# Self-attention: the order of TensorE's work over two key tiles, and the lag of the weighings

## The chip, the cores and the metric

The program runs on one core of one Trainium2 chip. The metric is the device time of one execution in microseconds. The engines are TensorE (PE, matmuls; PEld is its weight load), VectorE (DVE), ScalarE (ACT), GpSimd (POOL) and SyncE (SP, which issues DMAs). Each runs its own queue in order and waits for semaphores of the others.

## The reference

The kernel computes two decoder layers on x (4 x 1024 tokens, width 256): cross-attention to 64 context tokens, self-attention with a mixture of experts, cross-attention again, and a second mixture of experts. The change is in the self-attention alone:

```python
q = (src @ q_w).reshape(b, s, h, hd).transpose(0, 2, 1, 3)
k = (src @ k_w).reshape(b, s, h, hd).transpose(0, 2, 1, 3)
v = (src @ v_w).reshape(b, s, h, hd).transpose(0, 2, 1, 3)
scores = jnp.einsum('bhqd,bhkd->bhqk', q, k) / np.float32(np.sqrt(hd))
scale = jax.nn.sigmoid(jnp.einsum('bhsd,hd->bhs', q, scale_w)) * 2.0
scores = scores * scale[..., None]
aw = jax.nn.softmax(scores, axis=-1)
out = jnp.einsum('bhqk,bhkd->bhqd', aw, v).transpose(0, 2, 1, 3).reshape(b, s, d)
```

Here b = 4, s = 1024, h = 16, hd = 16.

## The kernel before

The stages of the program are separate blocks that run one after the other. An earlier stage stores queries (with their scale) and keys in bf16 parts. `self_attention` takes 16 groups of four heads (one batch each) and halves the queries of a group: 32 units of 512 queries by 1024 keys by 4 heads. `n` is the unit, `kt` its key tile (8 tiles of 128 keys), `head` 0 to 3.

In a unit each engine does this:

- TensorE, scores (line 1137): for each key tile and head one matmul, 128 keys by 512 queries, over 112 partitions, into one of three PSUM buffers `bps`. The partitions hold the bf16 parts of queries and keys and two rows with the negated maximum of each query, so the maximum is already taken off. There are four a tile.
- ScalarE, exponentials (line 1086): one for each of these, out of PSUM into `ex`, of which there are two buffers, one for each key tile in turn.
- TensorE, weighings (line 1147, `weigh_values`): once a tile, the four heads' 17 columns of values (16 and a column of ones for the sum) times their exponentials. The heads stand side by side in 32 columns of the array each, and each fp32 matmul shows as two instructions, so eight a tile. They add up in the one buffer `ops` over the unit.
- TensorE, maxima (line 1106, `first_scores`): rougher scores of a unit to come, 128 queries by 1024 keys, on 48 partitions. Two heads run at a time, one on partitions 0 to 47 and one on 64 to 111, into one of two buffers `aps`. VectorE takes the maximum of each (line 1020). A unit needs 16 such steps, two a tile; they run a unit and more ahead (`ahead` says for which).
- In tile 3 (`MAX_AT`) TensorE transposes the next unit's maxima (line 1118), ScalarE copies them negated (line 1064), GpSimd splits them (line 982) and SyncE sends them through memory into the rows of the queries.
- When a unit's last weighing is done, ScalarE copies `ops` (line 1056, `keep_out`) in the next unit's first tile. In tile 5 (`OUT_AT`) TensorE transposes the copy (line 1127), ScalarE copies the result (line 1072) and GpSimd divides (line 993).

The order of each queue is written out by hand in the `body` of each engine. On TensorE a tile is: score 0, two maximum steps, a transpose if one is due, score 1, the weighing of the tile before, scores 2 and 3. The transposes use the same three PSUM buffers as the scores, in turn (`b_use`). Semaphores of the part: `b_filled` (a score buffer is written), `b_used` (ScalarE has read it), `a_filled` and `a_used` (the same for maxima), `pv_done` (weighings done), `o_evacuated` (`ops` copied). A score waits for the exponential three buffers back:

```python
def fill(use):
    if use >= 3:
        pe.wait_ge(b_used, use - 2)
```

Of the kernel before, what the change touches and what calls it, by code (L numbers as in the profile page):

```python
# [13 lines left out]
P = 128  # L14
# [8 lines left out]
CW = CT * P  # L23
# [557 lines left out]
GH = 4  # L581
# [268 lines left out]
def self_attention(nc, attn, ident, q_parts, k_parts, v_dram, m_dram, x_sb, n2_b):  # L850
# [10 lines left out]
    MAX_AT, OUT_AT = 3 * GH + 1, 5 * GH + 1  # L861

# [18 lines left out]
    with ExitStack() as ctx:  # L881
# [5 lines left out]
        ex = [sb(f"e{i}", [P, GH, CW]) for i in range(2)]  # L887
# [30 lines left out]
        with nc.Block() as block:  # L918
# [133 lines left out]
            def _(act):  # L1052
# [21 lines left out]
                def body(g, turn, s, turn1, s1):  # L1074
                    for qc in range(2):
                        n = 2 * g + qc
                        for i in range(GH * KT):
# [19 lines left out]
            def _(pe):  # L1097
# [42 lines left out]
                def weigh_values(n, kt, s, turn):  # L1140
# [5 lines left out]
                    for head in range(GH):  # L1146
                        last = nc.tensor.matmul(ops[32 * head:32 * head + VW], vs[s][:, kt, head], ex[kt % 2][:, head],  # L1147
                                                start=(kt == 0), stop=(kt == KT - 1))
                    last.then_inc(pv_done, 1)

                def body(g, turn, s, turn1, s1):
                    for qc in range(2):
                        n = 2 * g + qc
                        for kt in range(KT):
                            scores(n, GH * kt, s, turn, qc)
                            for which in range(2):
                                if ahead(n, kt, which):
                                    a, k = ahead(n, kt, which)
                                    if kt < 2 and qc == 0:
                                        first_scores(a, k, s, turn, 1)  # L1160
                                    else:
                                        first_scores(a, k, s1, turn1, 0 if kt < 2 else qc)
                            if GH * kt + 1 == MAX_AT and n + 1 < UNITS:
                                transpose_max(n + 1)
                            if GH * kt + 1 == OUT_AT and n >= 1:
                                transpose_out(n)
                            scores(n, GH * kt + 1, s, turn, qc)
                            if kt:
                                weigh_values(n, kt - 1, s, turn)
                            elif qc:  # L1170
                                weigh_values(n - 1, KT - 1, s, turn)
                            elif g >= 1:
# [1497 lines left out]
```

## Time and profile before

| | us |
|---|---|
| median of 3 runs | 2056.4 (2055.46 to 2056.41) |
| the profiled execution, its own time | 2058.98 |
| its span | 2056.9 |
| TensorE, VectorE, ScalarE, GpSimd busy over the span | 1713.4, 1250.0, 969.1, 603.5 |
| scores: 1024 matmuls | 311.1 |
| weighings: 2048 | 270.4 |
| maxima: 1024 matmuls, 512 reductions | 168.2, 602.3 |
| exponentials: 1024 | 534.5 |

A matmul's time in the profile is from its start to a modelled end, and neighbours overlap. So the distance from start to start says what one costs TensorE, not the duration. Reductions and exponentials overlap their neighbours in the same way, a little. A row that groups several instructions gives the start of the first and the time that all together cover.

### The profile page before, as it was taken

What the parts mean: (1) busy time and instruction counts of PE and PEld (TensorE: products, weight loads), DVE (VectorE), ACT (ScalarE), POOL (GpSimd) and SP (SyncE); (2) the same over time, 40 slices, a digit from 0 to 9 for tenths busy, and PEclk for the clock granted to TensorE, in tenths of its full rate; (3) what the DMA queues carried; (4) which work ended last, traced back from release to release, by engine and by line L of the source; (5) the groups of instructions that cost most, each with busy time, mean ns of one, the idle gap of its engine ahead of it and who ended that gap; (6) DMA issues with size and microseconds to landing.
All of it is one profiled execution on the core that took longest, in us unless ns stands there. A gap on an engine that the chain in (4) does not pass through costs nothing. (4 is left out here: it accounts for less than half of the span.)

```text
span 2056.9 us, 30275 instructions
## 1 busy us (share of the span) xinstructions
PE 1713.4 (83%) x10579; PEld 808.6 (39%) x10580; DVE 1250.0 (61%) x2123; ACT 969.1 (47%) x1811; POOL 603.5 (29%) x645
## 2 busy tenths in 40 slices
PE   5799799389999999999997884999077996329997
PEld 3466455012222222222221563776044663125654
DVE  5344344588888888888881484665783554562221
ACT  3422256158888888888887331444242332102110
POOL 4300034613222122121122264666561001120533
PEclk9899989679999999999999995999588998758998
DMA  5000048711221111321100622221400003310542
GB/s 138 1 2 1 16 156 288 208 38 38 55 56 38 38 38 38 67 45 37 38 2 1 220 80 85 59 69 56 125 1 1 1 1 124 135 32 11 124 122 31
DMA packets 112675, 134.48 MB, mean 65 GB/s; under 512 B 18481, under 2 KB 88497, under 8 KB 112273
## 3 DMA queue, kind: packets, MB, share of 16 engines
q1 hardware_dynamic: 101824, 114.20, 20.5%
q0 software_dynamic: 9552, 17.83, 3.6%
q8 instruction: 86, 1.41, 0.3%
q10 hardware_dynamic: 1152, 0.54, 0.1%
q14 instruction: 61, 0.49, 0.1%
HBM read 78.47 MB, written 53.93 MB: 64 GB/s over the span
## 5 line engine op out<-in xcount | busy, mean ns | idle before, releaser
L1020 DVE TENSOR_REDUCE sa_mhalf<-sa_a 128x2 f32<-128x1024 f32 x512 | 602.3, 1221 | 86.8 <-PE sa_a L1106 86.8
L1086 ACT ACTIVATE sa_e<-sa_b 128x512 f32<-128x512 f32 x1024 | 534.5, 601 | 139.4 <-PE sa_b L1137 139.4
L1137 PE MATMUL sa_b<-sa_q,sa_k 112*128 112x512 bf16 x1024 | 311.1, 385 | 3.2 <-ACT sa_e L1086 3.0
L1147 PE MATMUL sa_ops<-sa_e,sa_v 128*17 128x512 f32 x2048 | 270.4, 599 | 6.3 <-ACT sa_e L1086 1.1
L1137 PEld LDWEIGHTS sa_b<-sa_q,sa_k 112*128 112x128 bf16 x1024 | 78.8, 97 | 322.6 <-ACT sa_e L1086 281.6
L1106 PE MATMUL sa_a<-sa_k,sa_q 48*128 48x512 bf16 x1024 | 168.2, 398 | 38.4 <-DMA sa_k<-k_parts 24.5
L993 POOL TENSOR_TENSOR sa_rden<-sa_o_rows,sa_minus_one 128x16 f32<-128x16 f32 x32 | 93.1, 2908 | 180.1 <-ACT sa_o_rows L1072 180.1
L213 DVE TENSOR_REDUCE xa_mx<-xa_rows 128x16 f32<-128x1024 f32 x64 | 78.3, 1224 | 102.6 <-PE xa_rows L445 102.6
L982 POOL CAST sa_negm<-sa_neg 16x128 bf16<-16x128 f32 x32 | 9.0, 281 | 380.1 <-issue 338.0
L1106 PEld LDWEIGHTS sa_a<-sa_k,sa_q 48*128 48x128 bf16 x1024 | 42.1, 93 | 177.6 <-issue 77.0
L360 ACT ACTIVATE xa_pT<-xa_cols 128x1024 f32<-128x1024 f32 x64 | 62.1, 1021 | 84.9 <-PE xa_cols L477 84.9
L2552 DVE TENSOR_TENSOR sw_hT<-sw_p,sw_act 128x512 f32<-128x512 f32 x32 | 22.1, 692 | 101.9 <-PE sw_p L2497 101.9
L2465 POOL DMA_INDIRECT out_x<-sw_yo,tc_idx x32 | 49.9, 1560 | 105.5 <-DVE sw_yo L2559 98.5
L1637 PE MATMUL ex_hps<-at_w,ex_xT 128*128 x156 | 77.3, 619 | 1.9 <-ACT ex_xT L1677 1.9
L445 PE MATMUL xa_rows<-xa_kblk,xa_qT 64*128 64x256 f32 x512 | 73.1, 407 | 6.1 <-DVE xa_mx L213 5.3
L2541 ACT ACTIVATE sw_act<-sw_p 128x512 f32<-128x512 f32 x32 | 19.1, 597 | 118.8 <-PE sw_p L2491 110.3
L1660 PE MATMUL ex_yps<-at_attn,ex_hT 128*128 x312 | 74.1, 380 | 0.5 <-ACT ex_hT L1687 0.4
L544 PE MATMUL xa_cols<-c_ctxT,c_wts 128*128 128x256 f32 x16 | 7.5, 652 | 78.0 <-PEq L43 64.5
L1687 ACT ACTIVATE ex_hT<-ex_tps,at_bt,at_g 128x128 f32<-128x128 f32 x156 | 58.8, 457 | 15.7 <-PE ex_tps L1648 15.7
L726 POOL TENSOR_TENSOR sp_var<-sp_mv,x_eps_pow 128x4 f32<-128x4 f32 x8 | 7.5, 939 | 190.7 <-DVE sp_mv L683 190.7
L2491 PE MATMUL sw_p<-sw_xT,tc_w 128*128 128x512 f32 x128 | 62.0, 608 | 1.2 <-ACT sw_xT L2530 1.2
L1147 PEld LDWEIGHTS sa_ops<-sa_e,sa_v 128*17 128x17 f32 x2048 | 34.9, 95 | 69.5 <-ACT sa_e L1086 48.8
(328 smaller groups left out, 2819.7 us busy)
## 6 DMA issues: line engine op xcount, KB each, us to landing
k_parts<-sp_kpart SPq DMA_DIRECT2D x96, 128.0 KB, 1.8
sa_q<-q_parts SPq DMA_DIRECT2D x64, 192.0 KB, 5.1
sa_k<-k_parts SPq DMA_DIRECT2D x64, 192.0 KB, 5.6
tc_w<-in_L_ffn_W SPq DMA_DIRECT2D x24, 512.0 KB
q_parts<-sp_qpart SPq DMA_DIRECT2D x16, 384.0 KB, 3.3
ex_xg<-expert_in SPq DMA_DIRECT2D x39, 132.0 KB
v_groups<-sp_vt SPq DMA_DIRECT2D x8, 544.0 KB, 4.1
sa_v<-v_groups SPq DMA_DIRECT2D x16, 272.0 KB, 7.3
```

The source lines that it names most:

```text
L213: nc.vector.tensor_reduce(mx[:, t], rows[:].rearrange("p r (n k) -> p (r n) k", k=SC), axis=X, op=ALU.max).then_inc(max_done, 1)
L360: nc.scalar.activation(pT[:, 4 * half + 2 * part:4 * half + 2 * part + 2], cols[:, 2 * part:2 * part + 2], ACT.Exp, scale=SCALE).then_inc( ...
L445: last = nc.tensor.matmul(rows[:, r, half * D:(half + 1) * D], qT[part, half, tokens], kblk[part, c // 2, half, CT * r:CT * (r + 1)], star ...
L993: nc.gpsimd.tensor_tensor(rden[:], view[:, :, :, DK], minus_one[:], ALU.pow).then_inc(rden_made, 1)
L1020: nc.vector.tensor_reduce(mhalf[a % 2][:, half, head:head + PAIRED + 1:PAIRED, t], aps[use % 2][:], axis=X, op=ALU.max).then_inc(a_used, 1)
L1086: nc.scalar.activation(ex[kt % 2][:, head], bps[use % 3][:], ACT.Exp, scale=SCALE).then_inc(b_used, 1)
L1106: last = nc.tensor.matmul(aps[use % 2][:, h // PAIRED], qs[s][rows, h, q0:q0 + P], ks[s][rows, h, half * CW:(half + 1) * CW], start=True, ...
L1137: nc.tensor.matmul(bps[use % 3][:], ks[s][:, head, kt * P:(kt + 1) * P], qs[s][:, head, qc * CW:(qc + 1) * CW], start=True, stop=True).the ...
L1147: last = nc.tensor.matmul(ops[32 * head:32 * head + VW], vs[s][:, kt, head], ex[kt % 2][:, head], start=(kt == 0), stop=(kt == KT - 1))
L1637: last = nc.tensor.matmul(hps[j % 2][:], xT[j % 2][:, half], ew["w1"][:, half, ds(e, 1), :], start=(half == 0), stop=(half == HALVES - 1))
L1660: last = nc.tensor.matmul(yps[j % 2][:, 0:D], hT[j % 2][:, f], ew["w2"][:, f, ds(e, 1), :], start=(f == 0), stop=(f == FK - 1))
L2491: last = nc.tensor.matmul(p1[f % 2][:], w1[e % 3][:, half, f * P:(f + 1) * P], xT[e % 2][:, half], start=(half == 0), stop=(half == HALVES ...
```

## The change

TensorE's order is written for two tiles at a time, and the weighing of a tile comes two tiles behind its exponentials (`LAG = 2`) in place of one. In an even tile: scores 0 and 1, the weighing, one maximum step, scores 2 and 3. In an odd tile: score 0, one maximum step, the weighing, a transpose if one is due, scores 1 and 2, two maximum steps, score 3. A third buffer of exponentials takes the tile more that is under way, and ScalarE's wait before it writes one goes one weighing further back. The copy of `ops` moves with the last weighing, from behind the second exponential of a unit to behind its sixth. Behind the last unit two weighings are left in place of one. What is computed, and how many instructions of each kind, is the same.

```diff
+    LAG = 2
...
-        ex = [sb(f"e{i}", [P, GH, CW]) for i in range(2)]
+        ex = [sb(f"e{i}", [P, GH, CW]) for i in range(LAG + 1)]
...
-                            if head == 0 and n >= 1 or kt >= 2 and head == 0:
-                                act.wait_ge(pv_done, KT * n + kt - 1)
+                            if head == 0 and KT * n + kt > LAG:
+                                act.wait_ge(pv_done, KT * n + kt - LAG)
                             act.wait_ge(b_filled, use + 1)
-                            nc.scalar.activation(ex[kt % 2][:, head], bps[use % 3][:], ACT.Exp, scale=SCALE).then_inc(b_used, 1)
-                            if i == 1 and n >= 1:
+                            nc.scalar.activation(ex[(KT * n + kt) % (LAG + 1)][:, head], bps[use % 3][:], ACT.Exp, scale=SCALE).then_inc(b_used, 1)
+                            if i == GH + 1 and n >= 1:
                                 keep_out(n)
...
-                            scores(n, GH * kt, s, turn, qc)
-                            for which in range(2):
-                                if ahead(n, kt, which):
...
-                            if GH * kt + 1 == MAX_AT and n + 1 < UNITS:
-                                transpose_max(n + 1)
-                            if GH * kt + 1 == OUT_AT and n >= 1:
-                                transpose_out(n)
-                            scores(n, GH * kt + 1, s, turn, qc)
-                            if kt:
-                                weigh_values(n, kt - 1, s, turn)
...
-                            for head in range(2, GH):
-                                scores(n, GH * kt + head, s, turn, qc)
+                            def maxima(pairs):
+                                for p in pairs:
+                                    if ahead(n, kt // 2 * 2 + p // 2, p % 2):
...
+                            if kt % 2 == 0:
+                                scores(n, GH * kt, s, turn, qc)
+                                scores(n, GH * kt + 1, s, turn, qc)
+                                weigh()
+                                maxima((0,))
+                                scores(n, GH * kt + 2, s, turn, qc)
+                                scores(n, GH * kt + 3, s, turn, qc)
+                            else:
+                                scores(n, GH * kt, s, turn, qc)
+                                maxima((1,))
+                                weigh()
+                                if GH * kt + 1 == MAX_AT and n + 1 < UNITS:
+                                    transpose_max(n + 1)
+                                if GH * kt + 1 == OUT_AT and n >= 1:
+                                    transpose_out(n)
+                                scores(n, GH * kt + 1, s, turn, qc)
+                                scores(n, GH * kt + 2, s, turn, qc)
+                                maxima((2, 3))
+                                scores(n, GH * kt + 3, s, turn, qc)
...
-                weigh_values(UNITS - 1, KT - 1, (GROUPS - 1) % SETS, (GROUPS - 1) // SETS)
+                for kt in range(KT - LAG, KT):
+                    weigh_values(UNITS - 1, kt, (GROUPS - 1) % SETS, (GROUPS - 1) // SETS)
```

TensorE in two plain tiles, before. `sa_b` is a score buffer, `sa_a` one of the maxima, `sa_ops` the weighing's, `sa_e` the exponentials that it reads; the numbers are those of the buffers.

```order
L1137 MATMUL sa_b0<-sa_q1,sa_k1 128x512
L1106 MATMUL sa_a0<-sa_k2,sa_q2 128x512 x2
L1106 MATMUL sa_a1<-sa_k2,sa_q2 128x512 x2
L1137 MATMUL sa_b1<-sa_q1,sa_k1 128x512
L1147 MATMUL sa_ops<-sa_e1,sa_v1 17x512 x4
L1137 MATMUL sa_b2<-sa_q1,sa_k1 128x512
L1137 MATMUL sa_b0<-sa_q1,sa_k1 128x512
L1137 MATMUL sa_b1<-sa_q1,sa_k1 128x512
L1106 MATMUL sa_a0<-sa_k2,sa_q2 128x512 x2
L1106 MATMUL sa_a1<-sa_k2,sa_q2 128x512 x2
L1137 MATMUL sa_b2<-sa_q1,sa_k1 128x512
L1147 MATMUL sa_ops<-sa_e0,sa_v1 17x512 x4
```

The same place now, from score 0 of an odd tile to the first maximum step of the even tile behind it (lines are one higher).

```order
L1138 MATMUL sa_b1<-sa_q1,sa_k1 128x512
L1107 MATMUL sa_a1<-sa_k2,sa_q2 128x512 x2
L1148 MATMUL sa_ops<-sa_e2,sa_v1 17x512 x4
L1138 MATMUL sa_b2<-sa_q1,sa_k1 128x512
L1138 MATMUL sa_b0<-sa_q1,sa_k1 128x512
L1107 MATMUL sa_a0<-sa_k2,sa_q2 128x512 x2
L1107 MATMUL sa_a1<-sa_k2,sa_q2 128x512 x2
L1138 MATMUL sa_b1<-sa_q1,sa_k1 128x512
L1138 MATMUL sa_b2<-sa_q1,sa_k1 128x512
L1138 MATMUL sa_b0<-sa_q1,sa_k1 128x512
L1148 MATMUL sa_ops<-sa_e0,sa_v1 17x512 x4
L1107 MATMUL sa_a0<-sa_k2,sa_q2 128x512 x2
```

The weighing stands beside a maximum step on both tiles' sides, and the score right ahead of the even tile's weighing (the last `sa_b0`) writes the buffer that the second score behind the odd tile's weighing (the first `sa_b0`) has filled.

ScalarE from the copy of the transposed output in one unit (L1072) to the negated maxima in the next (L1064), before:

```order
L1072 ACTIVATE sa_o_rows<-sa_b 128x512
L1086 ACTIVATE sa_e<-sa_b 128x512 x13
L1056 ACTIVATE sa_o<-sa_ops 128x512
L1086 ACTIVATE sa_e<-sa_b 128x512 x11
L1064 ACTIVATE sa_neg<-sa_b 16x128
```

And now:

```order
L1073 ACTIVATE sa_o_rows<-sa_b 128x512
L1087 ACTIVATE sa_e<-sa_b 128x512 x17
L1057 ACTIVATE sa_o<-sa_ops 128x512
L1087 ACTIVATE sa_e<-sa_b 128x512 x7
L1065 ACTIVATE sa_neg<-sa_b 16x128
```

The copy of `ops` (L1056, now L1057) has moved four exponentials back, into the unit's tile 1.

## Rows read from the trace of the kernel before

**Rows 1.** The page, part 1: busy time, share of the span, instructions.

```profile
PE 1713.4 (83%) x10579; PEld 808.6 (39%) x10580; DVE 1250.0 (61%) x2123; ACT 969.1 (47%) x1811; POOL 603.5 (29%) x645
```

**Rows 2.** Busy time by stretch; below, all matmuls of line 1106.

```profile
core 0: us, PE busy (x) PEld busy (x) DVE busy (x) ACT busy (x) POOL busy (x), PEclk, DMA share, GB/s
500.00:1000.00 500.00, 496.79 (x3046) 121.84 (x3043) 435.73 (x389) 405.61 (x802) 109.08 (x97) 1.00 0.22 43
...
L1106 PE MATMUL sa_a<-sa_k,sa_q x1024: 376/386/631, 392.4 to 1085.0; 48*128 48x512 bf16 x171
```

**Rows 3.** Timeline of TensorE, tiles 2 and 3 of a unit.

```profile
start us, us, engine line op out<-in xcount [idle before <-releaser]
...
693.64 0.82 PE L1137 MATMUL sa_b<-sa_q,sa_k 112*128 112x512 bf16 x3
694.39 0.61 PE L1106 MATMUL sa_a<-sa_k,sa_q 48*128 48x512 bf16 x4
694.93 0.39 PE L1137 MATMUL sa_b<-sa_q,sa_k 112*128 112x512 bf16 x1
695.25 1.05 PE L1147 MATMUL sa_ops<-sa_e,sa_v 128*17 128x512 f32 x8
696.24 0.82 PE L1137 MATMUL sa_b<-sa_q,sa_k 112*128 112x512 bf16 x3
696.99 0.64 PE L1106 MATMUL sa_a<-sa_k,sa_q 48*128 48x512 bf16 x4
697.56 0.28 PE L1118 MATMUL sa_b<-x_ident,sa_mfull 128*16 128x128 f32 x1
697.80 0.39 PE L1137 MATMUL sa_b<-sa_q,sa_k 112*128 112x512 bf16 x1
698.12 1.05 PE L1147 MATMUL sa_ops<-sa_e,sa_v 128*17 128x512 f32 x8
699.11 0.82 PE L1137 MATMUL sa_b<-sa_q,sa_k 112*128 112x512 bf16 x3
```

**Rows 4.** Waits from 440 to 1080 us: who waited for whom, total, times, longest.

```profile
PEld sa_b L1137 <- ACT sa_e L1086: 255.3, 413, 0.9
```

**Rows 5.** Timeline of the last unit, which has no maxima left.

```profile
1099.30 1.05 PE L1147 MATMUL sa_ops<-sa_e,sa_v 128*17 128x512 f32 x8
...
1100.28 0.82 PE L1137 MATMUL sa_b<-sa_q,sa_k 112*128 112x512 bf16 x3
...
1100.71 2.06 ACT L1086 ACTIVATE sa_e<-sa_b 128x512 f32<-128x512 f32 x4 [0.48 <-PE sa_b L1137]
...
1101.36 0.39 PE L1137 MATMUL sa_b<-sa_q,sa_k 112*128 112x512 bf16 x1 [0.26 <-ACT sa_e L1086]
...
1101.85 1.05 PE L1147 MATMUL sa_ops<-sa_e,sa_v 128*17 128x512 f32 x8
```

**Rows 6.** Timeline of VectorE at the tiles of rows 3; the page's group of line 1020.

```profile
694.83 2.36 DVE L1020 TENSOR_REDUCE sa_mhalf<-sa_a 128x2 f32<-128x1024 f32 x2 [0.27 <-PE sa_a L1106]
697.42 2.36 DVE L1020 TENSOR_REDUCE sa_mhalf<-sa_a 128x2 f32<-128x1024 f32 x2 [0.24 <-PE sa_a L1106]
...
L1020 DVE TENSOR_REDUCE sa_mhalf<-sa_a 128x2 f32<-128x1024 f32 x512 | 602.3, 1221 | 86.8 <-PE sa_a L1106 86.8
```

**Rows 7.** Timeline of TensorE in the second cross-attention, at two places.

```profile
1618.26 1.13 PE L445 MATMUL xa_rows<-xa_kblk,xa_qT 64*128 64x256 f32 x8
1619.32 1.92 PE L486 MATMUL xa_front<-xa_pT,xa_vblk 128*32 128x512 f32 x16
...
1618.80 0.60 PE L445 MATMUL xa_rows<-xa_kblk,xa_qT 64*128 64x256 f32 x4
...
1653.74 1.13 PE L445 MATMUL xa_rows<-xa_kblk,xa_qT 64*128 64x256 f32 x8
1654.80 1.92 PE L486 MATMUL xa_front<-xa_pT,xa_vblk 128*32 128x512 f32 x16
```

**Rows 8.** Timeline of ScalarE, then TensorE, around the output's transpose, tile 5.

```profile
702.13 1.08 ACT L1086 ACTIVATE sa_e<-sa_b 128x512 f32<-128x512 f32 x2 [0.53 <-PE sa_b L1137]
...
703.72 0.60 ACT L1072 ACTIVATE sa_o_rows<-sa_b 128x512 f32<-128x512 f32 x1
704.22 0.59 ACT L1086 ACTIVATE sa_e<-sa_b 128x512 f32<-128x512 f32 x1
...
701.71 0.82 PE L1137 MATMUL sa_b<-sa_q,sa_k 112*128 112x512 bf16 x3
...
703.03 0.66 PE L1127 MATMUL sa_b<-x_ident,sa_o 128*128 128x128 f32 x4
703.52 0.38 PE L1137 MATMUL sa_b<-sa_q,sa_k 112*128 112x512 bf16 x1
...
704.82 0.39 PE L1137 MATMUL sa_b<-sa_q,sa_k 112*128 112x512 bf16 x1
```

**Rows 9.** Timeline of ScalarE and TensorE around the output copy.

```profile
712.78 0.60 ACT L1056 ACTIVATE sa_o<-sa_ops 128x512 f32<-128x512 f32 x1 [0.24 <-PE sa_ops L1147]
713.27 2.06 ACT L1086 ACTIVATE sa_e<-sa_b 128x512 f32<-128x512 f32 x4
...
712.64 0.82 PE L1137 MATMUL sa_b<-sa_q,sa_k 112*128 112x512 bf16 x3
...
715.48 0.39 PE L1137 MATMUL sa_b<-sa_q,sa_k 112*128 112x512 bf16 x1
```

**Rows 10.** Line 1056 between 690 and 760 us: count, durations, first and last start.

```profile
L1056 ACT ACTIVATE sa_o<-sa_ops x4: 597/598/598, 690.9 to 756.5; 128x512 f32<-128x512 f32 x4
```

**Rows 11.** The first weighing, timeline of TensorE, and busy times and clock there.

```profile
430.10 1.91 PE L1147 MATMUL sa_ops<-sa_e,sa_v 128*17 128x512 f32 x8
431.94 0.89 PE L1137 MATMUL sa_b<-sa_q,sa_k 112*128 112x512 bf16 x3
...
429.00:432.50 3.50, 3.50 (x16) 0.48 (x12) 2.53 (x3) 1.13 (x3) 0.00 (x0) 0.55 0.00 0
```

**Rows 12.** Timeline of TensorE at the end of the stage.

```profile
1125.46 1.05 PE L1147 MATMUL sa_ops<-sa_e,sa_v 128*17 128x512 f32 x8 [0.96 <-ACT sa_e L1086]
1127.23 0.66 PE L1127 MATMUL sa_b<-x_ident,sa_o 128*128 128x128 f32 x4 [0.72 <-ACT sa_o L1056]
```

**Rows 13.** Timeline of ScalarE at the tiles of rows 3.

```profile
696.66 1.57 ACT L1086 ACTIVATE sa_e<-sa_b 128x512 f32<-128x512 f32 x3 [0.53 <-PE sa_b L1137]
```

More of the change, by code:

```diff
@@ L1146, in weigh_values @@
                     for head in range(GH):
-                        last = nc.tensor.matmul(ops[32 * head:32 * head + VW], vs[s][:, kt, head], ex[kt % 2][:, head],
+                        last = nc.tensor.matmul(ops[32 * head:32 * head + VW], vs[s][:, kt, head], ex[(KT * n + kt) % (LAG + 1)][:, head],
                                                 start=(kt == 0), stop=(kt == KT - 1))
@@ L1154, in body @@
                         for kt in range(KT):
-                            scores(n, GH * kt, s, turn, qc)
-                            for which in range(2):
-                                if ahead(n, kt, which):
[L1158 to L1162, printed above, removed]
@@ L1163, in body @@
-                            if GH * kt + 1 == MAX_AT and n + 1 < UNITS:
-                                transpose_max(n + 1)
-                            if GH * kt + 1 == OUT_AT and n >= 1:
-                                transpose_out(n)
-                            scores(n, GH * kt + 1, s, turn, qc)
-                            if kt:
-                                weigh_values(n, kt - 1, s, turn)
-                            elif qc:
-                                weigh_values(n - 1, KT - 1, s, turn)
-                            elif g >= 1:
-                                weigh_values(n - 1, KT - 1, (s - 1) % SETS, turn)
@@ L1174, in body @@
-                            for head in range(2, GH):
-                                scores(n, GH * kt + head, s, turn, qc)
+                            def maxima(pairs):
+                                for p in pairs:
+                                    if ahead(n, kt // 2 * 2 + p // 2, p % 2):
+                                        a, k = ahead(n, kt // 2 * 2 + p // 2, p % 2)
+                                        if kt < 2 and qc == 0:
+                                            first_scores(a, k, s, turn, 1)
+                                        else:
+                                            first_scores(a, k, s1, turn1, 0 if kt < 2 else qc)
@@ new lines, in weigh @@
+                            def weigh():
+                                if kt >= LAG:
+                                    weigh_values(n, kt - LAG, s, turn)
+                                elif qc:
+                                    weigh_values(n - 1, KT + kt - LAG, s, turn)
+                                elif g >= 1:
+                                    weigh_values(n - 1, KT + kt - LAG, (s - 1) % SETS, turn)
+                            if kt % 2 == 0:
[5 more added lines that the diff above has]
+                                scores(n, GH * kt + 3, s, turn, qc)
+                            else:
+                                scores(n, GH * kt, s, turn, qc)
[9 more added lines that the diff above has]
+                                scores(n, GH * kt + 3, s, turn, qc)
```

## Prediction, made before the changed kernel ran

> Short names: s is one score matmul (line 1137), A one maximum step (two matmuls of line 1106 side by side), W one weighing (eight of line 1147), M and T the transposes of lines 1118 and 1127. s0E to s3E are the scores of an even key tile, s0O to s3O those of an odd one.
>
> **What bounds the kernel now.** I read the page's busy shares first, then the self-attention stretch alone, then the order of instructions in one key tile, and last the release of each wait. Over the whole span no engine is full, but in the 500 us inside self-attention TensorE is busy 496.8 us at full clock, VectorE 435.7, ScalarE 405.6 [rows 1, 2]. The stage's first matmul of maxima starts at 392.4 and its last transpose at 1127.2 [rows 2, 12]; its neighbours are separate blocks, so what it gains or loses moves the end one for one.
>
> A plain key tile repeats every 2.60 us (693.64 to 696.24), and TensorE's starts account for all of it [rows 3]. Three s then A: 0.75. The three s span 0.82 with a last one of 0.38, so s to s is 0.22 and s to A 0.31. The pair of A spans 0.61 with 0.38 each, so A to A is 0.23 and A to s 0.54 - 0.23 = 0.31. s to W is 0.32 and W to s 0.99; the second half of W starts 0.45 after the first in a 1.05 span of 0.60 each, so about 0.10 of the 0.99 is not streaming. Sum: 0.44 + 0.31 + 0.23 + 0.31 + 0.32 + 0.99 = 2.60. Thus each change of kind costs about 0.09 to 0.10 above the 0.22 that neighbours of one kind take, four times a tile. The table of waits blames ScalarE for 255 us before the scores [rows 4]; that is weight loading that stands behind W, not an idle TensorE, as the 496.8 us show.
>
> A second loop is almost as long: W waits for the tile's last exponential, s2 comes after W, and its exponential 0.43 after s2. Where no maxima are left it is alone and takes 2.55 (1099.30 to 1101.85) [rows 5]. So the lag of two frees a path that is only 0.05 shorter than TensorE's own. VectorE has slack: two reductions take 2.36 and it idles 0.24 before the next two [rows 6].
>
> **The change, part by part.** *TensorE's order.* Two tiles before: four s to s, two s to A, two A to A, two A to s, two s to W, two W to s = 0.88 + 0.62 + 0.46 + 0.62 + 0.64 + 1.98 = 5.20. After: s0E s1E W A s2E s3E s0O A W s1O s2O A A s3O. That is five s to s (1.10), s to W 0.32, W to A, A to s 0.31, s to A 0.31, A to W, W to s 0.99, s to A 0.31, A to A 0.23, A to s 0.31. Eight changes of kind before, eight after. Two boundaries are not in this loop's trace. A to W: in cross-attention, pairs of matmuls on 64 rows are followed by four at a time on 32 columns, the same two layouts. The last two pairs (x4, span 0.60, one 0.38) start 0.22 apart and the next kind 0.52 after the first of them, which leaves 0.30 to 0.31 [rows 7]; from the first of the four pairs it is 1.06 in both places shown. Bounds: 0.23 (A to A, nothing extra) and 0.32 (s to W). I take 0.31. W to A: bounds 0.89 (two halves of 0.45, nothing extra) and 0.99 (W to s); above, one more 0.10. I take 0.99, since every other change of kind pays. Sum 5.18: the new order itself wins 0.02 in two tiles. VectorE keeps up with it: a reduction starts 0.44 after its A (694.39, 694.83) and the next 1.14 behind (2.36 - 1.22) [rows 3, 6], so the first two, with A at 1.53 and 2.59, start at 1.97 and 3.11; the second ends at 4.33, before the last A at 4.65 that writes its buffer.
>
> *The lag and the third buffer.* W no longer waits for ScalarE and ScalarE's guard on the buffers is a weighing long past: nothing on the path. But the score buffers are still three. s1 of an even tile may only be written when the exponential of s2O is done, and s2O stands close behind s1O, right after W. Chain from s1E: W 0.32, A 0.99, s2E 0.31, s3E and s0O 0.44, A 0.31, W 0.31, s1O 0.99 = 3.67; exponential of s1O 0.43 later, that of s2O 0.48 behind it (two span 1.08, one 0.60) [rows 5, 8], its length 0.60, and 0.05 until the score matmul that waits for it (1100.71 + 0.60 to 1101.36) [rows 5]. Total 5.23. That beats 5.18 and is 0.03 over 5.20: **+0.03 per two tiles, +0.12 per unit** of eight.
>
> The Trainium skill's page TensorEngine Tiling (Array Packing), section PSUM Bottleneck, says that packing speeds up TensorE but not the emptying of PSUM. The trace agrees so far: 5.18 on TensorE stands against 5.23 on ScalarE's side.
>
> *The output copy* (line 1056) moves from behind the exponential of s1E in tile 0 to behind that of s1O in tile 1. There it sits inside the chain just named: copy to next exponential is 0.49 (712.78 to 713.27) [rows 9], so the exponential of s2O, and s1 of tile 2 with it, come 0.49 later. Before, the copy cost that unit 0.24: the tile from 712.64 to 715.48 takes 2.84 [rows 9]. **+0.25 per unit.** Its own wait is gone (0.24 idle [rows 9]), since s1O comes 0.99 after W; that wins nothing, for the exponential it stands behind starts later than W ends.
>
> *M* at tile 3: before 2.87 against 2.60, +0.27 [rows 3]; after it stands between W and s1O and adds M to s, 0.24. **-0.03.**
>
> *T* at tile 5: before the tile takes 3.11 (701.71 to 704.82), +0.51 [rows 8]. After, T to s adds 0.49. Then ScalarE copies the rows 0.69 after T's start and takes 0.50 to the next exponential, at 1.19; that exponential could have started 0.49 + 0.43 = 0.92 after T. The 0.27 was absorbed before, behind W; now it lies in the chain: 0.76. **+0.25.**
>
> Sum per unit: 0.12 + 0.25 - 0.03 + 0.25 = +0.59. Units 1 to 29 of 32 have all of it: 29 x 0.59 = **+17.1**. A unit before is (756.5 - 690.9) / 3 = 21.87 us long, from four output copies [rows 10].
>
> *Ends.* In unit 0 the first W leaves tile 1, where W to s took 1.84, with a granted clock of 0.55, so mostly at the level of 1.2 GHz [rows 11], and nothing of the output costs applies: **-1.8**. The maxima there are held by VectorE, so I take no more. From tile 2 of unit 30 on there are no A, seven tile pairs. Before 5.10 each [rows 5]; after, the chain from s1E to s1O is 0.32 + 0.99 + 0.44 + 0.32 + 0.99 = 3.06, plus 1.56 = 4.62: 7 x -0.48 = -3.4. The dearer output copy and T, two of each, give back 2 x 0.25 + 2 x 0.25 = 1.0: **-2.4**. The final second W fits into the 0.96 that TensorE idles for the last exponential [rows 12].
>
> Total 17.1 - 1.8 - 2.4 = +12.9. The profiled execution took 2058.98 us (span 2056.9 and 2.1 around it) and would take 2071.9; the timed runs have the median 2056.4, so I put **2069.3 us**. About 0.2% (4 us) is what a measurement of this kernel can tell from no change.
>
> **The rivals.** *A: W and A next to each other cost no change.* Then W to A is 0.89 and A to W 0.23, 0.18 less per two tiles; 121 such pairs have both, 12.9 - 21.8 = -8.9: 2047.5 us. For it: both are packed layouts and W now waits for nothing. Against it: rows 7; and s to W reads 0.32 even behind M, where the exponential it needs, the second of 696.66, ended about 0.4 us earlier (W at 698.12) [rows 3, 13]. The Trainium skill's page TensorE: Matmul & The Clock Gate, section The mechanism (Part 3), says that weight loads are pulled ahead of running matmuls when row groups do not conflict or the background buffer is free. By that, weights would be loaded early and this rival's time holds. Its page TensorEngine Tiling (Array Packing), section Key Properties, says instead that changing the tiling mode drains the engine; by that my 0.31 and 0.99 hold, and rows 7 stand on that side.
>
> *B: only one of the two is free.* -0.10 or -0.08 on 121 pairs: 12.9 - 11 = about +2: 2058.3, no change.
>
> *C: the chain over the three score buffers does not bind,* because exponentials release earlier than I read. Then TensorE's 5.18 sets the pace and output copy and row copy are hidden: 4 x 5.18 + 0.24 + 0.49 = 21.45 against 8 x 2.60 + 0.24 + 0.27 + 0.51 = 21.82 a unit, 29 x -0.37 = -10.7. Seven pairs without A take 6 x 0.22 + 2 x 0.32 + 2 x 0.99 = 3.94 for 5.10, -8.1, unit 0 -1.8: -20.6, 2035.8 us. Against it: rows 5 show just this release, 0.05 behind the exponential.
>
> *D: W to A costs one change more, A to W too.* +0.20 on 121 pairs: +24, 2093.5 us. Only that no row shows W to A speaks for it.
>
> **How the numbers follow.** Forecast 0.78, A 0.07, B 0.06, C 0.04, D 0.05. The forecast's own spread is 2063 to 2076: 0.05 us in either direction on the chain of two tiles is 6 us. Range 2057 to 2078: it takes in B and leaves A, C and D out. Faster 0.11; same 0.08 (B and the low edge of the forecast); slower 0.81.
>
> **What would show it.** Right: eight changes of kind in two tiles, W to A near 0.99 and A to W near 0.31; two plain tiles at 5.2, the even short (about 2.3) and the odd long (about 2.9); an idle of TensorE before s1 of tile 2, about 0.5 behind the output copy, and one behind T; unit 22.4 us; weighings never waiting; the last unit shorter by 1 to 2 us. Wrong: A to W near 0.23, or no idle of TensorE before s1 of the even tiles, or maxima waiting for VectorE in the doubled place (A A), which by rows 6 have over 0.2 us to spare.

## The result and the profile after

The changed kernel took 2065.72 us, median of 7 runs (2063.00 to 2068.61), against 2056.40 for the kernel before (7 runs). The ratio is 1.0050, interval 1.0038 to 1.0062: slower, by 9.3 us. The forecast was 2069.3 us, range 2057 to 2078. One execution of a later run, e5_short_exp_before, took 4343.41 us where its others took 2029.01 to 2030.16; it counts as slow and is left out there.

The spans of the two profiled executions differ by 7.0 us (2056.9, 2063.9), the self-attention stage by more. From its first maximum matmul to its last transpose it took 1127.23 - 392.4 = 734.8 us before [rows 2, 12] and takes 1134.10 - 387.7 = 746.4 now: +11.6. The stages ahead of it, whose code did not change, happened to take 4.7 us less in this execution, those behind it 0.1 more. So the stage is the steadier measure, and below each run is also given by it. It is not free of chance either: how much of its first unit falls before TensorE's clock rises moves it by about 1 us (see *Unit 0* below).

Line 1107 in the trace after (all its matmuls: min, median, max, first and last start), and the end of the stage in TensorE's timeline:

```profile
L1107 PE MATMUL sa_a<-sa_k,sa_q x1024: 376/386/631, 387.7 to 1096.2; 48*128 48x512 bf16 x171
...
1132.33 1.05 PE L1148 MATMUL sa_ops<-sa_e,sa_v 128*17 128x512 f32 x8 [0.25 <-ACT sa_e L1087]
1134.10 0.66 PE L1128 MATMUL sa_b<-x_ident,sa_o 128*128 128x128 f32 x4 [0.72 <-ACT sa_o L1057]
```

The stretch of [rows 2], after: TensorE is busy 489.41 of 500 us and not 496.79, at the same full clock, and the other engines do less as well.

```profile
500.00:1000.00 500.00, 489.41 (x2981) 114.53 (x2977) 424.56 (x381) 400.11 (x783) 108.35 (x95) 1.00 0.22 42
```

TensorE's timeline from tile 5 of one unit to tile 0 of the next answers to [rows 3]:

```profile
704.04 0.66 PE L1128 MATMUL sa_b<-x_ident,sa_o 128*128 128x128 f32 x4
704.54 0.60 PE L1138 MATMUL sa_b<-sa_q,sa_k 112*128 112x512 bf16 x2
705.07 0.61 PE L1107 MATMUL sa_a<-sa_k,sa_q 48*128 48x512 bf16 x4
705.60 1.15 PE L1138 MATMUL sa_b<-sa_q,sa_k 112*128 112x512 bf16 x3
706.69 1.05 PE L1148 MATMUL sa_ops<-sa_e,sa_v 128*17 128x512 f32 x8
707.67 0.39 PE L1107 MATMUL sa_a<-sa_k,sa_q 48*128 48x512 bf16 x2
707.99 0.82 PE L1138 MATMUL sa_b<-sa_q,sa_k 112*128 112x512 bf16 x3
708.75 0.39 PE L1107 MATMUL sa_a<-sa_k,sa_q 48*128 48x512 bf16 x2
709.07 1.05 PE L1148 MATMUL sa_ops<-sa_e,sa_v 128*17 128x512 f32 x8
710.05 0.60 PE L1138 MATMUL sa_b<-sa_q,sa_k 112*128 112x512 bf16 x2
710.59 0.61 PE L1107 MATMUL sa_a<-sa_k,sa_q 48*128 48x512 bf16 x4
711.13 0.88 PE L1138 MATMUL sa_b<-sa_q,sa_k 112*128 112x512 bf16 x3
711.94 1.05 PE L1148 MATMUL sa_ops<-sa_e,sa_v 128*17 128x512 f32 x8
712.92 0.39 PE L1107 MATMUL sa_a<-sa_k,sa_q 48*128 48x512 bf16 x2
```

Both unseen boundaries are there. Weighing to maximum step: 706.69 to 707.67, 0.98. Maximum step to weighing: 708.75 to 709.07, 0.32. So neighbours of these two kinds pay for the change like all others. Two plain tiles take 5.25 (707.67 to 712.92). Three scores in a row span 0.82 where nothing holds them (707.99), 0.88 ahead of the even tile's weighing (711.13) and 1.15 behind the output's transpose (705.60). What is over 0.82 is TensorE waiting for a score buffer.

Before the change two plain tiles took 5.23, not twice the 2.60 of [rows 3]: 704.82 to 707.42 is 2.60, 707.42 to 710.05 is 2.63.

```profile
704.82 0.82 PE L1137 MATMUL sa_b<-sa_q,sa_k 112*128 112x512 bf16 x3
705.57 0.60 PE L1106 MATMUL sa_a<-sa_k,sa_q 48*128 48x512 bf16 x4
...
707.42 0.82 PE L1137 MATMUL sa_b<-sa_q,sa_k 112*128 112x512 bf16 x3
708.17 0.64 PE L1106 MATMUL sa_a<-sa_k,sa_q 48*128 48x512 bf16 x4
...
710.05 0.82 PE L1137 MATMUL sa_b<-sa_q,sa_k 112*128 112x512 bf16 x3
```

In every other tile the second maximum step started 0.25 behind the first and not 0.23, always 0.06 behind the end of the reduction that frees its buffer: a small wait for VectorE. The changed kernel has none, its two neighbouring steps are 0.23 apart everywhere.

The output copy in tile 1, ScalarE and TensorE:

```profile
693.37 0.60 ACT L1087 ACTIVATE sa_e<-sa_b 128x512 f32<-128x512 f32 x1 [0.48 <-PE sa_b L1138]
693.86 0.59 ACT L1057 ACTIVATE sa_o<-sa_ops 128x512 f32<-128x512 f32 x1
694.34 2.07 ACT L1087 ACTIVATE sa_e<-sa_b 128x512 f32<-128x512 f32 x4
...
694.02 0.60 PE L1138 MATMUL sa_b<-sa_q,sa_k 112*128 112x512 bf16 x2
695.00 0.39 PE L1138 MATMUL sa_b<-sa_q,sa_k 112*128 112x512 bf16 x1 [0.38 <-ACT sa_e L1087]
```

Score 0 of tile 2 starts at 694.24 (the second of 694.02), score 1 not before 695.00. It waits for the exponential of 694.34, whose 0.60 end at 694.94. The table of TensorE's own waits (PE) from 430 to 1080 us has this one, once in each of 29 units, and no other; before the change it had none:

```profile
PE sa_b L1138 <- ACT sa_e L1087: 10.9, 29, 0.4
```

The delay behind the output's transpose (704.04 on TensorE) shows only in ScalarE's starts. The row copy comes 0.70 behind the transpose, the exponentials 0.49 behind the copy; the second of them starts 0.48 later, ends 0.60 after that, at 706.31, and the last score of the group of 705.60 follows 0.05 behind:

```profile
704.74 0.60 ACT L1073 ACTIVATE sa_o_rows<-sa_b 128x512 f32<-128x512 f32 x1 [0.75 <-PE sa_b L1128]
705.23 1.57 ACT L1087 ACTIVATE sa_e<-sa_b 128x512 f32<-128x512 f32 x3
```

### The profile page after: what moved, and what is told of

Its sections match the earlier page's. It is cut to its first block and busy times, and to the rows that moved or that the text cites. A ratio compares the mean times of both kernels' runs of the same rounds, so it can differ in the third digit from the quotient of the medians.

```text
span 2063.9 us, 30275 instructions
## 1 busy us (share of the span) xinstructions
PE 1715.5 (83%) x10580; PEld 801.1 (39%) x10580; DVE 1248.3 (60%) x2123; ACT 975.0 (47%) x1811; POOL 603.2 (29%) x645
## 5 line engine op out<-in xcount | busy, mean ns | idle before, releaser
L1138 PE MATMUL sa_b<-sa_q,sa_k 112*128 112x512 bf16 x1024 | 306.5, 386 | 16.9 <-ACT sa_e L1087 12.9
L1107 PE MATMUL sa_a<-sa_k,sa_q 48*128 48x512 bf16 x1024 | 185.3, 398 | 37.8 <-DMA sa_k<-k_parts 24.5
L514 PE MATMUL xa_front<-c_wts,xa_oS 128*128 128x256 f32 x256 | 62.6, 400 | 2.6 <-DVE xa_oS L228 2.6
```

The costliest lines, as they stand in the source:

```text
L514: last = nc.tensor.matmul(front[:, bank, (t % 2) * D:(t % 2 + 1) * D], oS[:, k, t * P:(t + 1) * P], wts[:, 3, k], start=(k == 0), stop=(k ...
L1107: last = nc.tensor.matmul(aps[use % 2][:, h // PAIRED], qs[s][rows, h, q0:q0 + P], ks[s][rows, h, half * CW:(half + 1) * CW], start=True, ...
L1138: nc.tensor.matmul(bps[use % 3][:], ks[s][:, head, kt * P:(kt + 1) * P], qs[s][:, head, qc * CW:(qc + 1) * CW], start=True, stop=True).the ...
```

## The experiments

Two theories stand against each other. **Chain:** the two scores right behind the odd tile's weighing fill buffers that the next even tile needs again before its weighing; the way over ScalarE back to them is longer than TensorE's own work. **Neighbours:** what a weighing beside a maximum step costs on TensorE decides. A third says that the lag or the buffer matters by itself. e1 to e4 ran on one chip (before: 2057.5), e5 to e8 on a second (before: 2043.4), e9 and e10 on a third (before: 2043.7), so ratios and stages are to be compared, not microseconds. The kernel before has a trace from the first result alone; that stages carry over between chips rests on e4 and e7, one order of TensorE on two chips, 720.6 and 721.0. The stage is from first maximum to last transpose; a unit is from its first score to that of the next, in the middle of the stage.

| kernel | median us | ratio, interval | stage us | unit us |
|---|---|---|---|---|
| before | 2056.4 | | 734.8 | 21.84 |
| changed | 2065.7 | 1.0050, 1.0038 to 1.0062 | 746.4 | 22.36 |
| e1_copy_later | 2056.2 | 0.9996, 0.9983 to 1.0010 | 735.3 | 22.03 |
| e2_lag_alone | 2050.7 | 0.9960, 0.9943 to 0.9977 | 727.1 | 21.63 |
| e3_short_exp | 2049.0 | 0.9962, 0.9942 to 0.9982 | 729.3 | 21.81 |
| e4_two_by_two | 2042.9 | 0.9940, 0.9922 to 0.9957 | 720.6 | 21.46 |
| e5_short_exp_before | 2029.6 | 0.9928, 0.9910 to 0.9946 | 721.5 | 21.50 |
| e6_six_changes | 2111.0 | 1.0326, 1.0308 to 1.0345 | 808.1 | 24.41 |
| e7_two_buffers | 2030.4 | 0.9935, 0.9922 to 0.9949 | 721.0 | 21.47 |
| e8_neighbours_kept | 2045.0 | 1.0001, 0.9992 to 1.0010 | 739.5 | 22.13 |
| e9_order_alone | 2131.0 | 1.0430, 1.0404 to 1.0455 | 827.9 | 24.89 |
| e10_guard_early | 2040.2 | 0.9982, 0.9965 to 0.9998 | 730.9 | 21.88 |

**e1_copy_later**, against the changed kernel:

```diff
-                            if i == GH + 1 and n >= 1:
+                            if i == GH + 2 and n >= 1:
                                 keep_out(n)
```

> The changed kernel with one edit: the copy of ops stands behind the exponential of s2O (index GH + 2) and no longer between those of s1O and s2O. Theory (the chain s1E to s1O to the exponential of s2O to the next s1E is what binds): the 0.49 us that s1 of tile 2 waited for goes, tile 2 falls from 2.83 to about 2.5 (the weighing of tile 2 then waits a little for the copy), a unit from 22.36 to about 22.0, and the kernel by 29 x 0.34 = about 10 us, to 2056. Rival (the copy costs ScalarE time wherever it stands, or TensorE's order is what costs): no change from 2065.7.

The stage lost 11.1 us, the kernel its whole disadvantage. Tile 2 fell from 2.83 to 2.50. The copy takes ScalarE as long as before; moved by one exponential it is out of the chain. That is the chain's first confirmation, and its size was forecast: 0.33 a unit, 9.4 us over units 1 to 29. Of the rest of the 11.1, 1.2 lies in unit 0, which has no such copy and was shorter by its clock (see *Unit 0* below).

**e2_lag_alone**, against the changed kernel (the order of a tile as before the change):

```diff
+                            scores(n, GH * kt, s, turn, qc)
+                            maxima((0, 1) if kt % 2 == 0 else (2, 3))
...
+                            scores(n, GH * kt + 1, s, turn, qc)
+                            weigh()
+                            scores(n, GH * kt + 2, s, turn, qc)
+                            scores(n, GH * kt + 3, s, turn, qc)
```

> The lag of two, the third buffer and the later copy, but TensorE's order within a tile as before the change (score 0, two maximum steps, score 1, the weighing, scores 2 and 3). Theory: changes of kind are the same eight in two tiles and s1 comes ahead of the weighing, so the chain over the three score buffers is short; plain tiles stay at 2.60, the output copy is hidden (before it cost 0.24 a unit), the last fourteen tiles without maxima fall from 2.55 to about 2.2. Sum -4 to -6 against before: 2051 to 2053. Rival (the lag itself costs, by one more exponential buffer or by later weighings): 2060 or more. Rival (the lag frees TensorE more than its starts show): under 2045.

Stage -7.7 against before, kernel -0.4%: a little more than forecast. Plain tiles stayed at 2.60 and 2.63, the copy's 0.21 a unit went (6.1 us), and the last two units gave 1.9, less than forecast: their tiles without maxima fell from 2.55 to 2.38 and not to 2.2. So the lag with its later copy is a small gain by itself, and what made the changed kernel slow is the order.

**e3_short_exp** and its control **e5_short_exp_before**. In both, with `SHORT = 384`:

```diff
-... activation(ex[...][:, head], bps[use % 3][:], ACT.Exp, scale=SCALE)
+... activation(ex[...][:, head, 0:SHORT], bps[use % 3][:, 0:SHORT], ACT.Exp, scale=SCALE)
```

> The changed kernel with exponentials over 384 of the 512 queries; the last 128 columns of the exponentials stay at 1, so a quarter of the softmax is left out. Each exponential is 0.107 us shorter, TensorE's and VectorE's work is the same. Theory (the chain through ScalarE binds): two plain tiles fall from 5.25 to TensorE's own 5.18 to 5.20, the tile behind the output copy from 2.83 to about 2.6, the one of T from 3.45 to 3.40, a unit by 0.6; the kernel by 18 to 22 us, to about 2045. Rival (TensorE's order itself costs the difference, ScalarE is only 80% busy): within 3 us of 2065.7.

> The control of e3_short_exp: the kernel before the change with exponentials over 384 of 512 queries (the other columns stay at 1, a quarter of the softmax is left out). Read by the length of the self-attention stage, first maximum matmul to last transpose, since the values that come out of it also change how much work the experts have. Theory: TensorE's starts bind the old order, so plain tiles stay at 2.60 and only the output copy (0.2 a unit) and the last fourteen tiles give something: the stage falls from 734.8 by 5 to 10 us, against 17 in the changed kernel. Rival (shorter exponentials help any order alike): by about 17.

With TensorE's order untouched, shorter exponentials took 17.1 us off the changed stage (18 to 22 were forecast for the kernel). Two plain tiles fell to 5.19, TensorE's own sum, and the tile behind the copy to 2.61. The timeline of TensorE from that kernel's tile 0, to be read against 711.13 and 711.94 above (three scores now span 0.82 ahead of the weighing; 732.81 to 733.79 is the same 0.98 from weighing to maximum step, 734.87 to 735.19 the same 0.32 back):

```profile
732.06 0.82 PE L1141 MATMUL sa_b<-sa_q,sa_k 112*128 112x512 bf16 x3
732.81 1.05 PE L1151 MATMUL sa_ops<-sa_e,sa_v 128*17 128x512 f32 x8
733.79 0.39 PE L1110 MATMUL sa_a<-sa_k,sa_q 48*128 48x512 bf16 x2
...
734.87 0.39 PE L1110 MATMUL sa_a<-sa_k,sa_q 48*128 48x512 bf16 x2
735.19 1.05 PE L1151 MATMUL sa_ops<-sa_e,sa_v 128*17 128x512 f32 x8
```

The control is less clean than expected. The old order gained 13.3 in the stage, where 5 to 10 were forecast and 17 by the rival. Its plain tiles did stay at 2.60 and 2.63. Of the gain 10.1 lies in two places of units 1 to 29 where the old order does wait for ScalarE: the copy (tile 2.84 to 2.63) and the tile of the maxima's transpose (2.87 to 2.73); 3.2 more came in the last two units. In tiles, e3 separates the theories; the sums alone would not have. The rest of these two times is not used. The stages behind took 5.6 and 14 us less than in the first profile, but e7 and e8, on the chip of e5 and with all values right, show the same 14; that other values reach the experts need not have cost or saved anything.

**e4_two_by_two**, the new lines against the changed kernel:

```diff
+                            weigh()
+                            scores(n, GH * kt, s, turn, qc)
...
+                            scores(n, GH * kt + 1, s, turn, qc)
+                            maxima((0, 1) if kt % 2 == 0 else (2, 3))
+                            scores(n, GH * kt + 2, s, turn, qc)
+                            scores(n, GH * kt + 3, s, turn, qc)
...
-                            if i == GH + 1 and n >= 1:
+                            if i == GH and n >= 1:
                                 keep_out(n)
```

> An order made for the chain: in each tile the weighing (two tiles behind), scores 0 and 1, a transpose if due, two maximum steps, scores 2 and 3; the output copy behind score 4's exponential, else as the changed kernel. Again eight changes of kind in two tiles, but two scores stand between any two longer pieces, so none of the three buffers is asked for early. Theory: plain tiles 2.60 as before, no wait for ScalarE, M and T cost 0.24 and 0.49, the output copy nothing: a unit 21.6 against 21.84, and shorter ends: -8 to -11 against before, 2046 to 2049. Rival (weighings right behind the last score of a tile wait for something else, or VectorE starves): 2056 or more.

The fastest: 0.6% under the kernel before (14.5 us, more than the 8 to 11 forecast) and 25.8 us of stage under the changed one, with the same instructions and the same eight changes of kind. Two plain tiles take 5.23 to 5.24, hardly less than the 5.25 of the changed kernel. What this order saves over it is mostly the output copy (0.48 a unit) and a third of a microsecond at the output's transpose, which no longer lie where a score waits for them. TensorE's timeline over the output copy (at 708.12 on ScalarE): scores go in twos of 0.61, and the weighings are 2.61 and 2.62 apart.

```profile
706.15 1.05 PE L1148 MATMUL sa_ops<-sa_e,sa_v 128*17 128x512 f32 x8
707.14 0.61 PE L1138 MATMUL sa_b<-sa_q,sa_k 112*128 112x512 bf16 x2
707.68 0.61 PE L1107 MATMUL sa_a<-sa_k,sa_q 48*128 48x512 bf16 x4
708.22 0.61 PE L1138 MATMUL sa_b<-sa_q,sa_k 112*128 112x512 bf16 x2
708.76 1.05 PE L1148 MATMUL sa_ops<-sa_e,sa_v 128*17 128x512 f32 x8
...
711.38 1.05 PE L1148 MATMUL sa_ops<-sa_e,sa_v 128*17 128x512 f32 x8
```

**e7_two_buffers**, against e4:

```diff
-        ex = [sb(f"e{i}", [P, GH, CW]) for i in range(LAG + 1)]
+        ex = [sb(f"e{i}", [P, GH, CW]) for i in range(2)]
...
-                            if head == 0 and KT * n + kt > LAG:
-                                act.wait_ge(pv_done, KT * n + kt - LAG)
+                            if head == 0 and KT * n + kt > 1:
+                                act.wait_ge(pv_done, KT * n + kt - 1)
```

> e4_two_by_two with two buffers of exponentials in place of three, and ScalarE's guard one weighing nearer; TensorE's order is the same. Theory (the weighing at a tile's start is over before the first exponential that writes its buffer): the same as e4_two_by_two within 2 us, 2041 to 2045, so neither the third buffer nor the name of the lag brings anything, only the place of the weighing. Rival (the buffer carries the gain): a wait of ScalarE for the weighing in every tile, 2048 or more.

Stage 721.0 against 720.6, ratio 0.9935 against 0.9940: the same. The third buffer brings nothing there. (The edit also takes the index of `ex` modulo 2 in both places; the microseconds of the forecast were for the first chip.)

**e6_six_changes**, the new lines (the order of one tile) against the changed kernel:

```diff
+                            scores(n, GH * kt, s, turn, qc)
...
+                            scores(n, GH * kt + 1, s, turn, qc)
+                            weigh()
+                            maxima((0, 1) if kt % 2 == 0 else (2, 3))
+                            scores(n, GH * kt + 2, s, turn, qc)
+                            scores(n, GH * kt + 3, s, turn, qc)
```

> Weighing and both maximum steps together in every tile: scores 0 and 1, weighing, two maximum steps, scores 2 and 3. Only six changes of kind in two tiles, so TensorE's own sum is about 0.2 lower, 5.0. Theory (what stands between two groups of scores must not outlast the three buffers, and both maximum steps together wait for VectorE): a tile takes about 2.9, a unit 24.3, the kernel 2115 to 2125. Rival (changes of kind are the price that counts): 21.2 a unit, 2040.

```profile
739.16 1.05 PE L1148 MATMUL sa_ops<-sa_e,sa_v 128*17 128x512 f32 x8
...
740.15 0.61 PE L1107 MATMUL sa_a<-sa_k,sa_q 48*128 48x512 bf16 x4
...
740.58 2.36 DVE L1021 TENSOR_REDUCE sa_mhalf<-sa_a 128x2 f32<-128x1024 f32 x2 [0.56 <-PE sa_a L1107]
...
740.69 0.82 PE L1138 MATMUL sa_b<-sa_q,sa_k 112*128 112x512 bf16 x3
741.11 2.06 ACT L1087 ACTIVATE sa_e<-sa_b 128x512 f32<-128x512 f32 x4 [0.86 <-PE sa_b L1138]
...
741.76 0.39 PE L1138 MATMUL sa_b<-sa_q,sa_k 112*128 112x512 bf16 x1 [0.26 <-ACT sa_e L1087]
...
742.09 1.05 PE L1148 MATMUL sa_ops<-sa_e,sa_v 128*17 128x512 f32 x8
```

Two changes of kind fewer in two tiles and 3.3% slower. The chain adds up to the tile: 0.99 from the weighing to the maxima, 0.54 to score 2, 0.42 to its exponential, 0.60 and 0.05 to score 1, 0.33 to the next weighing = 2.93 (739.16 to 742.09). The half of the expectation that had VectorE in it was wrong: VectorE idles 0.56 ahead of its two, and TensorE does not wait for it.

**e8_neighbours_kept**, against the changed kernel:

```diff
                             if kt % 2 == 0:
                                 scores(n, GH * kt, s, turn, qc)
-                                scores(n, GH * kt + 1, s, turn, qc)
                                 weigh()
                                 maxima((0,))
+                                scores(n, GH * kt + 1, s, turn, qc)
                                 scores(n, GH * kt + 2, s, turn, qc)
                                 scores(n, GH * kt + 3, s, turn, qc)
                             else:
-                                scores(n, GH * kt, s, turn, qc)
                                 maxima((1,))
                                 weigh()
+                                scores(n, GH * kt, s, turn, qc)
...
                                 scores(n, GH * kt + 1, s, turn, qc)
+                                maxima((2, 3))
                                 scores(n, GH * kt + 2, s, turn, qc)
-                                maxima((2, 3))
                                 scores(n, GH * kt + 3, s, turn, qc)
```

> The changed order with weighings and maximum steps still next to each other, but a score moved in each tile: even tile score 0, weighing, maximum, scores 1 to 3; odd tile maximum, weighing, scores 0 and 1, two maximum steps, scores 2 and 3. Eight changes of kind, the same pairs of neighbours. Theory (the changed kernel is slow because of where the scores stand to their buffers, not by what a weighing beside a maximum step costs): no wait of TensorE for ScalarE before score 1, two plain tiles 5.2 to 5.25, the output copy nearly free, a unit 21.6 to 21.8, the stage 722 to 726 and the kernel 2044 to 2049. Rival (the neighbours themselves cost): 22.2 a unit or more, 2060.

A miss: 22.13 a unit, near the rival's 22.2, and 5.30 for two plain tiles. But not by the neighbours, whose boundaries read 0.98 and 0.32 here too. I had not followed the chain to its new place. Behind the odd tile's weighing now stand scores 0 and 1. Score 0 of the next even tile, right ahead of that tile's weighing, needs the buffer of score 1, whose exponential comes behind that of score 0; the way is as long as before. And it is 0.06 longer than its parts: the exponential behind score 0 starts late. TensorE, then ScalarE, in tiles 0 and 1:

```profile
735.39 0.60 PE L1138 MATMUL sa_b<-sa_q,sa_k 112*128 112x512 bf16 x2
...
735.88 1.08 ACT L1087 ACTIVATE sa_e<-sa_b 128x512 f32<-128x512 f32 x2 [0.54 <-PE sa_b L1138]
```

From the score's start to the exponential's it is 0.49, where the forecast's 0.43 was read at score 2.

**e10_guard_early**, against e8:

```diff
-                            if head == 0 and KT * n + kt > LAG:
-                                act.wait_ge(pv_done, KT * n + kt - LAG)
+                            if head == 2 and KT * n + kt >= LAG:
+                                act.wait_ge(pv_done, KT * n + kt + 1 - LAG)
```

> e8_neighbours_kept with ScalarE's wait for an old weighing moved from the first exponential of a tile to the third of the tile before; its condition is long fulfilled in either place. In e8 two plain tiles took 5.30, not 5.23, and the first exponential of a tile starts 0.49 us after its score where the others start 0.43 after. Theory (a second wait in front of an instruction costs 0.06 even where it is fulfilled, and that exponential lies in the chain from the scores behind a weighing to the next tile's score 0): 5.24 a pair, the stage 7 us shorter than the 739.5 of e8. Rival (the 0.06 belongs to the buffer or to the weighing beside it): no change of the stage.

Two plain tiles went to 5.24, a unit from 22.13 to 21.88. The stage lost 8.6 us, 7.2 of it in units 1 to 29 and 1.0 in unit 0, whose clock rose earlier in the unit here. (The two ran on different chips, so the tiles are the surer measure.) The same pair in this kernel:

```profile
755.15 0.61 PE L1138 MATMUL sa_b<-sa_q,sa_k 112*128 112x512 bf16 x2
...
755.58 1.08 ACT L1087 ACTIVATE sa_e<-sa_b 128x512 f32<-128x512 f32 x2 [0.48 <-PE sa_b L1138]
```

0.43 again. And the 0.06 went where the wait went: in the odd tiles score 2, whose exponential now carries it, starts at 707.14 and its exponential at 707.62. That is 0.49 in every such tile but the one with the output copy; in e4, where the exponential of score 2 has one wait, it is 0.43 and that of score 0, with two, 0.49. So the 0.06 were the second wait's.

**e9_order_alone**, against the changed kernel:

```diff
-    LAG = 2
+    LAG = 1
...
-                            if i == GH + 1 and n >= 1:
+                            if i == 1 and n >= 1:
                                 keep_out(n)
```

> The changed order of TensorE with the lag, the buffers and the output copy of before (lag 1, two buffers, copy behind the second exponential). Theory: the odd tile's weighing now stands one maximum step behind score 0 and waits for the fourth exponential of the tile before, with score 1 to 3 queued behind it; the even tile's weighing likewise. Two plain tiles take about 6.1 in place of 5.25, a unit 25.1, the kernel about 70 us more than the changed one, near 2120 on a chip where before is 2050. Rival (the lag is worth only the 0.05 us by which the old loop was shorter than TensorE's own): within 5 us of the changed kernel.

6.10 for two plain tiles and 24.89 a unit, as forecast; the total was 81 us of stage over the changed kernel and not 70, since 29 units of 2.5 make 73.5 and the last two units another 7.4. The changed order lives on the lag: TensorE stands 0.51 before the odd tile's weighing.

```profile
746.69 0.39 PE L1107 MATMUL sa_a<-sa_k,sa_q 48*128 48x512 bf16 x2
747.59 1.05 PE L1148 MATMUL sa_ops<-sa_e,sa_v 128*17 128x512 f32 x8 [0.51 <-ACT sa_e L1087]
```

## Why the prediction was right, point by point

The sum was +12.9 us for the stage; it came to +11.6.

| term | forecast | measured |
|---|---|---|
| weighing to maximum, maximum to weighing | 0.99, 0.31 | 0.98, 0.32 |
| two plain tiles | 5.20 to 5.23, +0.12 a unit | 5.23 to 5.25, +0.10 |
| output copy | +0.25 a unit | 0.21 to 0.48, +0.27 |
| M | -0.03 | 0.24 to 0.11, -0.13 |
| T | +0.25 | 0.48 to 0.76, +0.28 |
| a unit | +0.59 | +0.52 (21.84 to 22.36) |
| units 1 to 29 | +17.1 | +15.0 |
| unit 0 | -1.8 | -0.6 |
| units 30 and 31 | -2.4 | -2.8 |

The costs of the single places are taken over plain tiles of the same parity (2.60 and 2.63 before, two for 5.25 after), so that they add up to the unit. The total came closer than its parts: 2.1 us too much in units 1 to 29 and 0.4 at the end stand against 1.2 too little in unit 0, and that offset is luck.

- **TensorE bound before.** Right but for 0.03: with quicker exponentials two plain tiles stay at 5.23 in the old order (e5) and stop at 5.19 in the new (e3). The forecast doubled the tile of 2.60 and took VectorE to have slack; in every other tile TensorE waited 0.02 for it.
- **The new order wins next to nothing on TensorE.** Right: 0.03 for the 0.02 forecast, and both unseen boundaries at the value taken. Rivals A and B fell with that, D too. All orders here pay about 0.10 at every change of layout. The Trainium skill's page TensorEngine Tiling (Array Packing), section Key Properties, says that changing the tiling mode drains TensorE. The traces agree with it by that 0.10; whether it is a drain or a weight load that cannot be hidden no run tells.
- **The chain over three score buffers.** Right in kind and 0.02 short in size. e3 shortened the chain and two tiles fell to TensorE's own sum, not below; e10 took 0.06 out of the chain of e8 and two tiles fell by 0.06; in e6 the links add up to the tile; e1 took the copy's link out, and tile 2 fell by 0.33 of its 0.49, since its weighing then waits for the copy. Rival C fell. The share of T rests on the timeline above; no run changed it alone.
- **M.** Mis-sized. I read the 0.24 from M to the next score as M's cost. It was a wait for the exponential of score 3, which started at 697.14 and ended 0.05 ahead of that score [rows 3, 13]. M itself takes 0.11 (after the change it starts at 698.68 and the next score at 698.80), and since it now stands behind the weighing that wait is gone. e5 shows the same in the old order: with shorter exponentials the 0.24 fell to 0.11. TensorE's own row of waits had none: this one showed only as a late start.
- **Unit 0.** Mis-sized by 1.2, and by the clock. The first weighing leaves tile 1 as said, but in this execution it fell into tile 2 while the granted clock was still 0.50, the level of 1.2 GHz, and again took 1.84 (426.51 to 428.35), with VectorE idle 1.63. In e1, whose unit 0 is the same work in the same order, the clock rose to 1.00 just as it began (432.04), and it took 1.06. The rise came 9.5 us into the unit in the changed kernel, 7.0 in e1 and 7.6 before; the unit took 23.29, 22.12 and 23.88. So -1.8 is what e1 gave. Why the rise came so late in the changed kernel no run tells. The changed kernel, then e1:

```profile
426.51 1.91 PE L1148 MATMUL sa_ops<-sa_e,sa_v 128*17 128x512 f32 x8
429.00 2.47 DVE L1021 TENSOR_REDUCE sa_mhalf<-sa_a 128x2 f32<-128x1024 f32 x2 [1.63 <-PE sa_a L1107]
426.50:428.30 1.80, 1.80 (x9) 0.15 (x8) 0.84 (x2) 0.84 (x2) 0.00 (x0) 0.50 0.00 0
...
432.04 1.12 PE L1148 MATMUL sa_ops<-sa_e,sa_v 128*17 128x512 f32 x8
432.30:434.00 1.70, 1.70 (x13) 0.31 (x5) 1.03 (x3) 0.72 (x3) 0.00 (x0) 1.00 0.00 0
```

- **The kernel's time.** 9.3 by the medians for 11.6 in the stage. The stages ahead scatter by 4.7 us between two profiles of the same code, and the profiled execution before was 2.6 above its median, so such a difference is no surprise; where the 2.3 went is not shown. That the runs of the changed kernel spread over 5.6 us is not explained.

## What to carry to other kernels

When several kinds of work share an in-order engine, write down for each small buffer who fills it, who frees it, and which instruction asks for it again; the longest such way, not the engine's own sum, may be the period. Few changes of kind and equal spacing pull against each other: here two scores between any two longer pieces beat the order with six changes (e6) by 0.6 us in two plain tiles. Against the changed order, which makes as many changes, spacing won nothing in plain tiles (5.24 for 5.25) and 0.9 a unit where copies and transposes come in. A copy on the second engine should stand where the exponential behind it is not the one that frees the next buffer: one place further was worth 0.33 us a unit, 9.4 in all.

## What the runs showed of the hardware

- A second wait in front of an exponential cost 0.06 us even where it had long been fulfilled: 0.49 for 0.43 from score to exponential, and the 0.06 moved with the wait (e8, e10); 7.2 us over 29 units.
- A change between the three layouts cost TensorE 0.09 to 0.11 us whichever two they are: 0.22 between two scores, 0.31 between a score and a maximum step, 0.32 from 48 rows to 32 columns, and 0.98 from 32 columns to 48 rows like 32 columns to the full array. Behind a change the first weight load starts with its matmul (707.99 both, changed kernel), between two scores it starts 0.22 ahead (708.00 for 708.22).
- Executions on different chips differed by 14 us for the same kernel before (2057.5 on one, 2043.4 and 2043.7 on two others), more than most of the effects here. In e7's profile the stages behind the self-attention took 13.7 us less than in the first profile of before, while the stage agreed with e4's to 0.4.
